# Test-time-training block on one core: padded gradients and later masked queries as scaled copies on ScalarE, and a gate before each piece of GpSimd's loop work

## The reference

```python
Z1 = xk @ W1_s + b1_s
grad = _ln_fused_l2_bwd(Z1, xv - xk, ln_w, ln_b)
Attn1 = jnp.tril(xq @ xk.swapaxes(-1, -2))
b1_bar = b1_s - jnp.tril(eta_mb) @ grad
Z1_bar = xq @ W1_s - eta_mb * Attn1 @ grad + b1_bar
W1_new = W1_s - (last_eta * xk).swapaxes(-1, -2) @ grad
b1_new = b1_s - jnp.sum(last_eta * grad, axis=-2, keepdims=True)
out = xq + _ln(Z1_bar, ln_w, ln_b)
```

## Time and profile before

| | |
|---|---|
| median of 3 runs | 288.38 us |
| span of the profiled execution | 288.0 us |
| VectorE busy | 254.3 us, 88% |
| TensorE busy | 234.8 us, 82% |
| GpSimd busy | 145.5 us, 51% |
| ScalarE busy | 135.8 us, 47% |
| granted TensorE clock, mean | 0.819 of full speed |
| GpSimd padding sgpad, 16 instructions | 19.1 us |
| GpSimd masked queries, 32 instructions | 18.9 us |
| GpSimd masks, 32 instructions | 34.8 us |
| GpSimd products, 32 instructions | 32.0 us |

### The profile page before, as it was taken

The page is one execution under the profiler, slowest core; times in us unless marked ns, Lnnn a source line. Parts: engine busy times, 40 slices in busy tenths (PEclk is TensorE's granted clock), DMA queues, the critical chain, the costliest instruction groups (busy, mean ns, idle before and its releaser), DMA issues.

```text
span 288.0 us, 5083 instructions
## 1 busy us (share of the span) xinstructions
PE 234.8 (82%) x1812; PEld 169.2 (59%) x1812; DVE 254.3 (88%) x500; ACT 135.8 (47%) x297; POOL 145.5 (51%) x150
## 2 busy tenths in 40 slices
PE   8389959694654999799837989969989699993793
PEld 6285326363433677577625757548768377872672
DVE  1865499999999999999999999997999999999842
ACT  1141252725036344565361552826473726399392
POOL 1820679207925568546075539383981416152334
PEclk9955989577865699999966985957999859999598
DMA  6955000030000120030002001200300033000002
GB/s 228 393 174 159 0 1 2 2 78 0 0 0 3 16 66 0 2 80 0 3 5 73 0 2 17 65 0 0 80 2 0 2 78 147 2 3 0 0 38 109
DMA packets 21543, 13.20 MB, mean 46 GB/s; under 512 B 10512, under 2 KB 19728, under 8 KB 21008
## 3 DMA queue, kind: packets, MB, share of 16 engines
q1 hardware_dynamic: 21088, 11.84, 13.8%
q10 hardware_dynamic: 432, 1.06, 1.0%
HBM read 11.02 MB, written 1.84 MB: 45 GB/s over the span
## 4 chain that ended last, share of the span: by engine, by line
DVE 60%; PE 16%; issue 10%; ACT 5%; POOL 5%; DMA 3%; DVEq 0%; POOLq 0%; SPq 0%; ACTq 0%
DVE pr L694 8%; DVE pr L747 7%; DVE dW L752 6%; DVE T L700 5%; DMA x_bt<-in_x_bt 3%; POOL hh L310 3%; PE bank L886 3%; DVE hb L725 2%; DVE S L715 2%; DVE hb L738 2%; DVE T L704 2%; DVE cf L729 2%; DVE sgb L741 2%; DVE S L727 2%; DVE hb L733 2%
## 5 line engine op out<-in xcount | busy, mean ns | idle before, releaser
L310 POOL TENSOR_TENSOR hh<-gate,upw 128x256 f32<-128x256 f32 x32 | 32.0, 1003 | 60.0 <-ACT upw L457 59.8
L264 POOL TENSOR_TENSOR A<-A,mask 128x256 f32<-128x256 f32 x32 | 34.8, 1090 | 26.1 <-ACT A L440 26.1
L694 DVE TENSOR_TENSOR pr<-KP,W 128x1152 f32<-128x1152 f32 x16 | 38.4, 2399 | 0.4 <-DVE QP L647 0.2
L972 PE MATMUL bank<-down,hT 128*128 128x256 f32 x128 | 37.2, 419 | 0.0
L953 PE MATMUL bank<-gup_hi,xnL_hi 128*128 128x512 f32 x64 | 33.0, 515 | 3.8 <-POOL xnL_lo L344 3.8
L962 PE MATMUL bank<-small,hh 128*128 128x128 f32 x64 | 14.9, 321 | 21.5 <-POOL hh L310 21.5
L924 PE MATMUL bank<-xqm,xkT 32*32 32x128 f32 x512 | 22.4, 303 | 10.3 <-ACT A L440 6.2
L953 PE MATMUL bank<-gup_hi,xnL_lo 128*128 128x512 f32 x64 | 28.6, 446 | 0.0
L953 PE MATMUL bank<-gup_lo,xnL_hi 128*128 128x512 f32 x64 | 28.5, 445 | 0.0
L446 ACT ACTIVATE rr<-rr 128x16 f32<-128x16 f32 x16 | 3.4, 215 | 51.8 <-DVE rr L713 51.8
L747 DVE TENSOR_TENSOR pr<-KP,sgb 128x1152 f32<-128x1152 f32 x15 | 26.4, 1761 | 0.5
(11 more groups left out here) (143 smaller groups left out, 541.3 us busy)
## 6 DMA issues: line engine op xcount, KB each, us to landing
wblk<-w_blocks SPq DMA_DIRECT2D x8, 512.0 KB, 4.0
x_bt<-in_x_bt SPq DMA_DIRECT2D x2, 512.0 KB, 6.7
sgpad<-in_gup SPq DMA_DIRECT2D x1, 1024.0 KB, 9.6
G<-in_gup SPq DMA_DIRECT2D x1, 1024.0 KB, 11.5
down<-in_down SPq DMA_DIRECT2D x1, 1024.0 KB, 6.3
xkT<-in_x_tok SPq DMA_DIRECT2D x1, 1024.0 KB, 4.9
out<-G SPq DMA_DIRECT2D x4, 256.0 KB, 2.5
wkv<-in_wkv ACTq DMA_DIRECT2D x1, 512.0 KB, 8.0
```

The lines of the kernel that those rows point to most:

```text
L264: pool.tensor_tensor(scores, scores, mask_bc, ALU.mult).then_inc(S_["masked"], 1)
L310: pool.tensor_tensor(hh[:, i % 2, :, :], gate[:, i % 2, :, :], upw[:, i % 2, :, :], ALU.mult).then_inc(S_["h"], 1)
L694: v.tensor_tensor(pr1[:, :].rearrange("p (d t c) -> p d t c", d=HD, t=K), kp.rearrange("p c t -> p t c").unsqueeze(1).broadcast_to([P, HD, ...
L972: ins = pe.matmul(bank[7][:, 0:HS], hT[:, i % 2, r, :], down[:, 2 * e + r, :], start=(e == 0 and r == 0), stop=(e == 3 and r == 1))
```

## The change

Padding and queries from group 2 on leave GpSimd for ScalarE. A padding is then four copies (128 x 32 x 8, one for each sequence) with a column of bmask as the scale, where GpSimd had two products of 128 x 512; the queries stay four instructions of 128 x 256, with a column of cmask as the scale. Both use the function Copy. The padding of group j - 1 stands ahead of the square root of step 2j (for the first group ahead of its second tile, for the second group behind the first three slots), and the queries of group j + 1 ahead of the Sqrt preload of step 2j + 1.

GpSimd waits in four places of each group from 1 on: until L694 of the first step is done, until L747 of it is done, and the same in the second step. Behind each wait stand one hidden product, then one mask. Before, the mask came ahead of the product. In the last step, which has no L747, the fourth wait is for the gradient (L741).

```diff
@@ GpSimd @@
-                if j >= 2:
-                    pool.wait_ge(S_["sc"], 4 * (j - 1))
+                pool.wait_ge(S_["qchc"], 2)
...
-            def pad_grads(j):
...
+            def window(j, i):
+
+                n = 2 * j + i // 2
+                if i % 2:
+                    pool.wait_ge(S_["sg"], 4 * n + (3 if n < 2 * NG - 1 else 2))
+                else:
+                    pool.wait_ge(S_["chain"], 16 * n + 1)
...
-                mask_scores(j, 1)
-                hidden_product(slot)
-                mask_scores(j, 2)
-                pad_grads(j - 1)
-                mask_scores(j, 3)
-                hidden_product(slot + 1)
-                mask_scores(j, 4)
-                for i in range(slot + 2, slot + SLOTS[j]):
+                for i in range(4):
+                    window(j, i)
+                    if i < SLOTS[j]:
+                        hidden_product(slot + i)
+                    mask_scores(j, i + 1)
+                for i in range(slot + 4, slot + SLOTS[j]):
                     hidden_product(i)
@@ ScalarE @@
+            def masked_queries(j):
+
+                act.wait_ge(S_["qchc"], 2 + 2 * (j // 4))
+                act.wait_ge(S_["sc"], 4 * (j - 1))
+                for h in range(4):
+                    act.activation(xqm[:, j % 2, :, :, h, :], xqT[:, :, :, GT * j:GT * j + GT], ACT.Copy,
+                                   scale=cmask[:, h:h + 1]).then_inc(S_["queries_a"], 1)
+
+            def pad_grads(j):
+
+                act.wait_ge(S_["sgT"], j + 1)
+                if j >= 2:
+                    act.wait_ge(S_["z"], 2 * (j - 1))
+                else:
+                    act.wait_ge(S_["split"], 3)
+                for b in range(B):
+                    act.activation(sgpad[:, j % 2, :, b, :], sgT[:, :].rearrange("p (h d) -> p h d", d=HD), ACT.Copy,
+                                   scale=bmask[:, b:b + 1]).then_inc(S_["sgp"], 1)
...
             for j in range(1, NG):
+                if j == 1:
+                    pad_grads(0)
                 if j > 2:
+                    pad_grads(j - 1)
                     step_std(2 * j)
...
                 if j > 1:
+                    if j + 1 < NG:
+                        masked_queries(j + 1)
                     preload_sqrt(2 * j)
                     step_std(2 * j + 1)
...
                 if j == 1:
+                    masked_queries(2)
+                    pad_grads(1)
 
                     preload_sqrt(3)
                     step_std(4)
...
+            pad_grads(NG - 1)
             norm_z(0)
@@ VectorE, end of a group @@
-                    v.wait_ge(S_["sgp"], 2 * j)
+                    v.wait_ge(S_["sgp"], j * 4)
@@ TensorE, group_end: all four copies are needed before the first product @@
-                        pe.wait_ge(S_["sgp"], 2 * j + hf + 1)
+                        pe.wait_ge(S_["sgp"], 4 * (j + 1))
```

More of the change, by code:

```diff
@@ L186, in build @@
             zero_w zero_d top hi split queries pair pair_done sc scored mask masked chain vrc rstd sg w w_saved w_loaded b_saved
-            sgT sgp z0 z zc gu gact h hTp hT y g
+            sgT sgp z0 z zc gu gact h hTp hT y g queries_a
             zg zv zs post0 ov os yn yTp yT o res fin out"""
@@ L296, in masked_queries @@
             def masked_queries(j):
-                pool.wait_ge(S_["qchc"], 2 + 2 * (j // 4))
-                if j >= 2:
-                    pool.wait_ge(S_["sc"], 4 * (j - 1))
+                pool.wait_ge(S_["qchc"], 2)
                 for h in range(4):
@@ L357, in _ @@
             for j in range(NG):
-                if 1 < j + 1 < NG:
-                    masked_queries(j + 1)
                 if j == 1:
@@ L369, in _ @@
                     continue
-                mask_scores(j, 1)
-                hidden_product(slot)
-                mask_scores(j, 2)
-                pad_grads(j - 1)
-                mask_scores(j, 3)
-                hidden_product(slot + 1)
-                mask_scores(j, 4)
-                for i in range(slot + 2, slot + SLOTS[j]):
+                for i in range(4):
[4 more added lines that the diff above has]
+                for i in range(slot + 4, slot + SLOTS[j]):
                     hidden_product(i)
                 slot += SLOTS[j]
-            pad_grads(NG - 1)
             for i in range(slot, NS):
@@ L920, in tile @@
                     q = i - 1
-                    pe.wait_ge(S_["queries"], 4 * (j + 1))
+                    if j < 2:
+                        pe.wait_ge(S_["queries"], 4 * (j + 1))
+                    else:
+                        pe.wait_ge(S_["queries_a"], 4 * (j - 1))
                     for hf in range(KC):
```

## The result

The changed kernel took **296.42 us** (median of four runs, 294.53 to 300.05); the kernel before, on the same chip, 288.72. The ratio is 1.0221 [1.0164, 1.0278]: **slower by 2.2%**, where 284.2 us and a range up to 292 were forecast.

The account below looks back on a forecast made before the run. VectorE's own instructions were taken to bound the loop, lengthened by collisions with GpSimd. 29.8 us saved, less 10.5, 4.8, 8.0 and 2.3, gave 4.2 us: 283.8, with 0.4 for the median 284.2 us; range 275.5 to 292.

Parts of the forecast that it names:

- the collisions: VectorE and GpSimd products excluding each other in steps 3 to 14: 29.8 us before, 10.5 us left after.
- 1.2 us a group: Collisions left in each of groups 3 to 7 with the gates, part of the 10.5 us left.
- a third of 29.8: Share of collisions from paddings and queries; if only that share goes, 20 us are left, the upper end.
- step 4: Copies ahead of slot 0 and the preload delay the square root to 106.0: a new VectorE wait of 4.8 us.
- the price of the copies: A set of four ScalarE copies takes 1.64 us, between 1.3 and 2.17; 14 sets make 23 us.
- It costs nothing: Padding ahead of the square roots of steps 6, 8, 10, 12, 14: no wait, 1.5 us of cover left.
- The third rival: Gates passed late: products over a us behind the gate run into L694; slower or no change, chance 0.1.
- steps 7, 9, 11 and 13: VectorE waits for the odd square roots: 1.9 in groups 3 and 4, 1.5 in 5, 2.0 in 6.
- the 0.7 of step 15: Wait of 0.7 us forecast in group 7, which has no queries; part of the 8.0 us.
- the tail: Behind the last gradient, product 27 to zs: VectorE waits 3.0 us, 0.7 comes back, 2.3 us lost.
- the profiled execution's own time: The median was taken to stand 0.4 us above the profiled execution, giving 284.2 us from 283.8.
- the second rival: ScalarE sets the pace: the kernel gets slower; chance 0.2.

Follow-up runs that it names:

- early_first: The change with group 2's queries and group 0's padding ahead of the second sigmoid, group 1's padding behind step 4's root; ratio 1.0212 to the kernel before, repeated 1.0189.
- late_pads: The change with paddings from group 2 on behind the even square root and the last behind norm_z; 295.0 us, ratio 1.0162 to the kernel before.
- change_warm: The change with eight idle TensorE products behind the first slot in groups 2 to 7; 304.1 us, ratio 1.0442 to the kernel before.
- change_again: The change run once more, unaltered, beside its variants; 295.3 us, ratio 1.0246 to the kernel before.
- one_gate_less: The change without the fourth gate of group 6; 293.3 us, no ratio given.
- mixed: Kernel before plus gates in groups 1 to 5, three in group 6; paddings 0 to 6 on ScalarE, later ones behind even square roots; 282.7 us, 0.9803.
- pads_in_gap: Kernel mixed with paddings 2 to 6 moved behind the fourth tile's scores; 278.2 us, ratio 0.9567 to the kernel before; again 278.3 us, 0.9634.

## Why the prediction was wrong

The miss in span is 292.5 - 283.8 = 8.7 us: 4.2 in steps 3 to 14, 4.7 from step 15 on (45.1 forecast, 49.8 measured), less 0.3 that came before step 3 (all rounded). The 4.2 are 7.2 of waits in steps 6 and 14 and 1.8 in steps 4 and 5, none of them forecast, less 3.1 in the odd steps from 7 on and 1.8 of collisions, where more was forecast than came.

**Right in the total: the collisions.** 10.5 us were to be left (the items named there add up to 11.4), 8.7 are, and VectorE's busy time fell by 19.1. The 1.2 us a group in the 10.5 is shown by no run: the 8.7 are a remainder over steps 3 to 14 and are not told apart by group. But the gates were given the larger part of this, and they have 5.2 of the 19.1; the copies alone take 13.9, where the step put a third of 29.8. The masks are at their shortest, L742 (before L727) has a mean of 201 ns against 424. **Right: step 4**, 4.83 us against 4.8, though another 1.1 us of waiting for the fill, 0.7 in step 5, was not seen. **Right: the price of the copies**, 1.69 us a set against 1.64 out of bounds of 1.3 and 2.17.

**Wrong: "It costs nothing"**, of the padding ahead of the square roots of steps 6, 8, 10, 12 and 14. The step said that the preload of the group before ends up to 2 us into the group and left 1.5 us of cover. For step 6 the trace of before says otherwise:

```profile
127.04 0.20 ACT L470 ACTIVATE warm<-eps 128x1 f32<-128x1 f32 x1
128.20 0.21 ACT L446 ACTIVATE rr<-rr 128x16 f32<-128x16 f32 x1 [0.96 <-DVE rr L713]
```

Group 3 had begun at 122.24, so the preload ended 5.0 us into it, with 0.96 us to spare for 1.7 us of copies; in steps 10 and 12 it ended 4.9 and 5.0 us into the group. In the change it ended 1.1, 2.1 and 1.0 us into the groups of steps 8, 10 and 12, as forecast, and these waited for nothing, but 7.9 us into those of steps 6 and 14. Behind a late product the loss is then the padding plus the lateness, 3.4 us in step 6 and 3.9 in step 14 (7.2 in all, with 0 forecast). The third rival had products come late and run into VectorE's, and step 6 is that (1.80 us instead of 0.72, begun 0.13 us behind VectorE's); step 14 is the gate itself, and there the trace of before, with 6.1 us to spare, gave no warning.

**Wrong in size: steps 7, 9, 11 and 13.** 7.3 us were forecast, 4.2 measured, and split otherwise (0, 0.6, 0.3, 3.3); the 0.7 of step 15 did not come. The 1.9, 1.5, 2.0 and 0.7 us a group that make up the 8.0 are shown by no run. In the trace of before TensorE took 9.6 us in group 3 and 11.4 in group 4 from the start of tile 2 to the transposes behind the third slot's products, at a granted 1.00 from 125 to 136 us in the one, and 0.50 from 148 to 153 and 0.56 from 152.65 to 157 in the other; what the odd steps of the change then waited are the figures just given. They swing, up to 5.2 each in early_first, and a figure for each couldn't have been had from two groups of one trace. Step 13 has a product that ran into VectorE's in it too:

```profile
211.63 2.40 DVE L709 TENSOR_TENSOR pr<-KP,W 128x1152 f32<-128x1152 f32 x1
```

```profile
211.71 2.93 POOL L308 TENSOR_TENSOR hh<-gate,upw 128x256 f32<-128x256 f32 x1 [7.70 <-DVE dW L767]
```

The gate had opened at 209.9, but upw was done only at 211.58, with TensorE at 0.64 of its clock from 205 to 210. The product came 0.08 us behind VectorE's and took 2.93 us instead of 0.72, and TensorE's transposes stood 1.0 us for it. Every profile here in which step 13 waits over 2 us has such a product in that step (1.7 to 3.0 us long); late_pads and change_warm, with 1.6 and 1.4, have none.

**Wrong: the tail**, 2.3 us forecast and 7.6 measured. The step followed ScalarE's list behind product 27 to zs and stopped there. That part held: L819 waited 3.26 us, 3.0 were forecast. What it left out is TensorE's list behind the same product, which the sum holds at nothing. Transposes, `group_end(6)`, `group_start(7)`, the half's bias and slot 29 had been done or begun ahead of the last gradient before, and now all stand behind the gate; zv waits 3.8 us for them (2.3 in change_again). Without the last group's gates the tail is 4.1 us shorter. With them but without the copies (gates_only) the tail is still 40.2.

**Wrong, without effect: the profiled execution's own time.** I took the span for it. In the runs of both kernels the time stands 1.8 to 2.1 us above its span, so the profiled execution of before was about 290 us long, some 1.4 above the median and not 0.4 below it. The forecast is still the median less 4.2 us (288.4 - 4.2).

Slower came by waits for ScalarE, as the second rival is named, but not by those of steps 7, 9, 11 and 13, which fell short of the forecast (4.2 against 7.3) instead of growing. The chance given to slower, 0.25, was too small because the waits were sought at the steps where copies were added before odd square roots and not along what the gates hold back.

What stays open: how much of step 13's 3.3 us is the clock; why one_gate_less and late_pads had their upw earlier in step 5, and with it no held product; and what the product ahead of the mask is worth alone.

## What to carry to other kernels

A gate that keeps two engines from colliding saves the collision and costs the delay of everything that stands behind the gated instruction in the other engines' lists; follow that list to its end on each engine, above all past the last iteration, where nothing is left to hide it. Work moved to an engine that is half idle costs its own duration if it stands ahead of something awaited, and nothing if it stands where that engine waits anyway: moving the same paddings from behind the square root into such a gap brought 282.7 us to 278.2 (mixed and pads_in_gap). Where long products of two engines can meet, look at which begins first: here 0.05 us ahead or 0.13 us behind went with 0.72 or 1.80 us for GpSimd's, and with 0 or 3.4 us of waiting in the next step.

## What the chip showed that I had not expected

A clean gain of 19.1 us in VectorE's work did not shorten the kernel at all, since it came back as waits. The granted clock of TensorE fell to 0.50 in early_first_2 behind a wait of 3.0 us and stayed at or near it from 150 to 160; in the change a wait of the same 3.0 us was followed by 0.76 in 155 to 160. Both had been granted 1.00 up to 150. TensorE had been busy 1.5 of 5 us ahead of the fall in the one (145 to 150) and 2.0 of 5 (150 to 155, at 0.90) in the other, so nearly equal pasts gave different clocks. The square root behind them was waited for 5.1 us in the one and 0.6 in the other, of which the clock's part, by the 10.4 and 7.3 us above, is an estimated 3.1. And where a product of GpSimd met one of VectorE, which of the two began first, by 0.05 or 0.13 us, went with 0 or 3.4 us of waiting in the next step.
